# Decay sums of a gated delta-rule layer from bfloat16 parts instead of float32, with POOL writing their rows a phase ahead

## The chip, the cores and the metric

The kernel runs on one core of one Trainium2 chip. The metric is the device time of one execution, in microseconds (us). Engines are named as in the profile: PE is TensorE, PEld its weight loads, DVE is VectorE, ACT is ScalarE, POOL is GpSimd, SP is SyncE, which here issues the DMAs.

## The reference

One decoder layer on `x` (8 sequences of 128 tokens, 256 channels): a gated delta-rule attention with 8 heads, then a WKV mixer, then a mixture of 12 experts. The change touches the first part alone, and there the log decays:

```python
g = -jnp.exp(A_log) * jax.nn.softplus(x @ Wa.T + dt_bias)      # (B, L, H)
def step(state, inp):                                          # 2 steps per token, decay at the first
    state = state * jnp.exp(g_t)[..., None, None]
    corr = jnp.einsum('bhk,bhkv->bhv', k_t, state)
    state = state + jnp.einsum('bhk,bhv->bhkv', k_t, (v_t - corr) * b_t[..., None])
    o_t = jnp.einsum('bhk,bhkv->bhv', q_t, state)
```

The kernel doesn't step. It works on all 256 steps of a sequence at once, by matrices, and needs for every pair of steps the exponential of the sum of the `g` between them. A product of a 0/1 matrix with a matrix of `g` (its "decay rows") makes these sums.

## The kernel before, in words

The work goes head by head, in phases. Phase h (from -1 to 8) holds up to three things at once: the projections, convolutions and matrices of head h+1 ("new"), the start of the solve of head h ("now") and the rest of the solve and the output of head h-1 ("old"). The order of the steps on each engine is written out by hand: `TENSOR_ORDER`, `VECTOR_ORDER` and `SCALAR_ORDER` (lines 77 to 86) for phases 0 to 5, `FIRST_...` (lines 90 to 94) for phase -1, `NEXT_...` for phase 6, `LAST_...` and `FINAL_...` for the last two. A step with a prime belongs to head h-1.

Steps on PE, in the order of a phase: `0` to `9` are ten projections (L1290, each 4 records of 128x512), whose tiles ACT copies with the first tap (L592) and DVE convolves in three steps (L888, `u` in its order). A projection waits until DVE has done the third step of the projection two before it. `dt0`, `dt1` and `dt2` are the decay sums (L1337/L1338 for the first two, four sequences each; L1333/L1334 for the third). `ca`, `cs`, `nrm` sum squares, `e1_*`, `e2_*` are the products of keys (L1340, L1343), and `vt*` transposes. `mt0'`, `mm'`, `my1'` (L1359, L1364) merge blocks of the inverse, `w1`, `r2`, `w2`, `o` (L1476, L1478, L1480, L1482) apply it, `wo` (L1470) is the output projection and `ga` (L1466) the gate.

A decay sum is two matmuls that add up in PSUM: a float32 one (`seg`, a 0/1 matrix, times `Gb`) and a bfloat16 one (`segb` times `futb`, which puts a huge negative number on steps of the future). ACT takes the exponential of each tile (L631, L633 for `dt0` and `dt1`, L623, L624 for `dt2`).

POOL writes `Gb` with one instruction per head: the mask `lower` times `gl` of the head, repeated (L522, in `decay_rows`). For head 0 it comes at the end of a chain of small instructions in phase -1 (L502 to L516), and four small instructions for `beta` follow it (L526 to L529), on which DVE waits before its `rb` (L904). For head h+1, POOL first waits for `dt2` of head h on PE, since `Gb` is one buffer. Then it waits for `ly'` (L1439) and `yd` of head h and zeroes half of `Yc` (L535), which SP needs before the next scatter. Since these waits stand in one queue, `Gb` of head 2 and later is written in the phase that uses it, just behind L535.

Meanwhile DVE solves 16x16 blocks by substitution: 15 rounds per head of a multiply (L946, in the order an `s`) and a subtract (L953, another `s`), each of which reads two tensors in SBUF and waits for the one before. They are spread among `u`, `my0'`, `my1'` (L982), `r2_0'` and `r2_1'` (L985). `w2_0'` on PE waits for `r2_0'`. A convolution step reads one tensor from PSUM and one from SBUF.

Of the kernel before, what the change touches and what calls it, by code (L numbers as in the profile page):

```python
# [16 lines left out]
ALU = mybir.AluOpType  # L17
# [5 lines left out]
P = 128  # L23
# [19 lines left out]
class Signal:  # L43
# [10 lines left out]
    def next(self, name):  # L54
# [37 lines left out]
                "e1_5 e2_2 e1_6 e1_7 e2_3 vt0 vt1 vt2 vt3").split()  # L92
FIRST_TENSOR_ORDER = ("0 1 2 3 4 5 6 7 8 dt0 dt1 9 dt2 ca cs nrm e1_0 e1_1 e2_0 e1_2 e1_3 e2_1 e1_4 e1_5 e2_2 e1_6 e1_7 "
                "e2_3 vt0 vt1 vt2 vt3").split()
# [52 lines left out]
def build(nc, x, ctxt, w_qkv, w_gate, conv_w, w_ba, w_o, a_log, dt_bias, o_norm, t_decay, t_first,  # L147
          gate_w, w13, w2, consts, masks, y_init, expand, out):
    with ExitStack() as ctx:
# [30 lines left out]

        seg = sb("seg", [P, 2, P])
        segb = sb("segb", [P, 2, P], BF16)
        futb = sb("futb", [P, P], BF16)
        wba = sb("wba", [P, KC, 24])
        beta = sb("beta", [P, CH, H])
        bsig = sb("bsig", [P, CH, 2, H])
        gl = sb("gl", [P, B, H])
# [3 lines left out]
        tokb = sb("tokb", [P, B, 16])  # L191
        twice = sb("twice", [P, NH, P])
        al = sb("al", [P, H])
# [10 lines left out]
        xn = Vn2[0][:, :, :].rearrange("p c d -> p (c d)").rearrange("p (b c) -> p b c", b=B)  # L204
        Gb = sb("Gb", [P, B, L])
        DT2 = sb("DT2", [P, B, 192])
# [24 lines left out]
        T64 = sb("T64", [P, CH, 64])  # L231
        W1 = sb("W1", [P, B, D])
        R2 = sb("R2", [P, B, D])
        W2 = R2
# [79 lines left out]
        s_sq = Signal(sem("squares_ready"), ["0", "1"])  # L314
        s_gb = Signal(sem("decay_rows_ready"), ["gb"])
        s_yi = Signal(sem("solve_started_from_identity"), ["yi"], 16)
# [49 lines left out]
        def _(sp):  # L366
# [3 lines left out]
            for (dst, src), name in zip(first, s_first.names):  # L370
                sp.dma_start(dst, src).then_inc(s_first.next(name), 16)
            loads = [(seg[:, :, :], consts.rearrange("k p n -> p k n")[:, 6:8, :]), (cm[:, :], masks),
                     (al[:, :], a_log), (dtb[:, :], dt_bias),
# [98 lines left out]
        def _(pool):  # L472
# [43 lines left out]
            gt(gl[:, :, :], po, rep(al[:, :].rearrange("p (o h) -> p o h", o=1), 1, B), ALU.mult).then_inc(s_preG.next("gl"), 1)  # L516
            pool.wait_ge(s_preG.sem, s_preG.at("gl"))

            def decay_rows(h):

                hs = bass.ds(h, 1) if not isinstance(h, int) else slice(h, h + 1)
                g.tensor_tensor(Gb[:, :, :], rep(lower.rearrange("p (o l) -> p o l", o=1), 1, B), rep(gl[:, :, hs], 2, L), ALU.mult).then_inc(s_gb.next("gb"), 1)  # L522

# [4 lines left out]
            pk(gt(beta[:, :, :], beta[:, :, :], bsig[:, :, 0, :], ALU.add))  # L528
            gs(beta[:, :, :], beta[:, :, :], 2.0, None, ALU.mult).then_inc(s_preG.next("bparity"), 1)  # L529
            for h in range(H - 1):  # L530
                pool.wait_ge(prep.fills.sem, prep.fills.at("dt2", h))
                decay_rows(h + 1)
                pool.wait_ge(post.fills.sem, post.fills.at("ly", h))
                pool.wait_ge(s_yd.sem, s_yd.at("yd", h))
                g.tensor_tensor(Yc[:, :, SUB:BLK], T16[:, :, SUB:BLK], T16[:, :, SUB:BLK], ALU.add).then_inc(s_z.next("z"), 1)  # L535
# [281 lines left out]
        def _(dve):  # L817
# [50 lines left out]
            def gates():  # L868

                dve.wait_ge(s_first.sem, s_first.at("w_ba"))  # L870
                dve.wait_ge(s_ld.sem, 16 * N_LD)
                v.tensor_copy(segb[:, :, :], cst[:, 4:6, :])
                ts(futb[:, :], lower, BIG, -BIG, ALU.mult, ALU.add)

                dve.wait_ge(s_preA.sem, s_preA.at("gexp"))
                lk(ts(sm[2][:, :, :], sm[1][:, :, :], 2.0, None, ALU.add))
                v.reciprocal(sm[2][:, :, :], sm[2][:, :, :]).then_inc(s_preD.next("rr"), 1)
# [351 lines left out]
        def _(pe):  # L1229
# [72 lines left out]
            def prepare(name, h):  # L1302
                if name == "dt0":

                    pe.wait_ge(s_gb.sem, s_gb.at("gb", h))
                elif name == "ca":
                    pe.wait_ge(s_sq.sem, s_sq.at("0", h))
                elif name == "cs":
                    pe.wait_ge(s_sq.sem, s_sq.at("1", h))
                elif name == "nrm":  # L1310
                    pe.wait_ge(prep.emptied("cs").sem, prep.emptied("cs").at("cs", h))
                elif name == "e1_0":
                    pe.wait_ge(s_si.sem, s_si.at("u5", h))
                elif name == "vt0":
                    pe.wait_ge(s_si.sem, s_si.at(f"u{NU - 1}", h))
# [15 lines left out]
                elif name == "dt2":  # L1331
                    o = ps[:, :].rearrange("p (b l) -> p b l", b=B)
                    mm(o, seg[:, 1, :], Gb[:, :, 64:L], start=True, stop=False)  # L1333
                    ins = mm(o, segb[:, 1, :], rep(futb[:, 64:L].rearrange("p (o l) -> p o l", o=1), 1, B), start=False, stop=True)  # L1334
                elif name[:2] == "dt":
                    o = ps[:, :].rearrange("p (b l) -> p b l", b=4)
                    mm(o, seg[:, 0, :], Gb[:, 4 * i:4 * i + 4, :], start=True, stop=False)  # L1337
                    ins = mm(o, segb[:, 0, :], rep(futb[:, :].rearrange("p (o l) -> p o l", o=1), 1, 4), start=False, stop=True)  # L1338
# [336 lines left out]
```

## Time and profile before

| | before |
|---|---|
| median of three runs | 609.71 us (607.98 to 609.97) |
| the profiled execution's own time | 603.35 us |
| its span, first to last instruction | 601.6 us |
| mean granted TensorE clock in it | 0.972 of full |
| busy: PE, DVE, ACT, POOL | 557.3, 455.2, 357.8, 38.3 us |
| length of phases 1 to 4, by L535 | 59.2 to 59.4 us each |

A row of instructions reads: start, duration, engine, line, operation, what it writes <- what it reads, shapes, count; behind it in brackets how long the engine was idle before it, and who released it. Durations of PE's matmuls reach to the modelled end of each, so a stream of them overlaps; its pace is the distance between starts. A float32 matmul has two records.

### The profile page before, as it was taken

The page shows a single profiled execution, that of the slowest core. Times are in us where ns is not written, and L with a number is a line of the kernel's source. Part 1 is how long each engine was busy: PE and PEld are TensorE (multiplying, and loading weights), DVE is VectorE, ACT ScalarE, POOL GpSimd, SP SyncE. Part 2 cuts the span into 40 slices and gives each one's busy share as a digit, 9 for nine tenths or more (in the row PEclk, how much of TensorE's full clock was granted, in tenths as well). Part 3 has the DMA queues.
Part 4 walks back from the last instruction along what each step waited for, and adds up shares of the span by engine and source line. Part 5 has one row for each costly group of instructions (what it writes and reads, how often), then busy time and mean ns, then how long its engine had stood idle before and what let it go on. Part 6 is the DMA issues. An engine that isn't in the chain of part 4 may idle for free.

```text
span 601.6 us, 15363 instructions
## 1 busy us (share of the span) xinstructions
PE 557.3 (93%) x6484; PEld 377.7 (63%) x6484; DVE 455.2 (76%) x1066; ACT 357.8 (59%) x559; POOL 38.3 (6%) x66
## 2 busy tenths in 40 slices
PE   8799889999999999999999999999998799668997
PEld 5445347576657665766576667666666688556646
DVE  5778997797778877887788778878796535589663
ACT  2684766594659466946694668465864144187351
POOL 5340000100010001000100010010000000100000
PEclk9989999999999999999999999999998699968999
DMA  6001021102110200020002101210013400000002
GB/s 166 2 20 31 21 63 25 23 10 40 41 22 11 69 10 22 13 68 11 21 14 66 12 20 17 65 13 19 2 36 70 127 3 12 1 0 1 2 0 70
DMA packets 49700, 18.63 MB, mean 31 GB/s; under 512 B 39100, under 2 KB 48352, under 8 KB 49632
## 3 DMA queue, kind: packets, MB, share of 16 engines
q1 hardware_dynamic: 49632, 17.66, 12.2%
q8 instruction: 51, 0.84, 0.6%
q14 instruction: 17, 0.14, 0.1%
HBM read 14.49 MB, written 3.15 MB: 29 GB/s over the span
## 4 chain that ended last, share of the span: by engine, by line
PE 75%; DVE 11%; ACT 7%; issue 2%; SPq 1%; DMA 1%; POOL 0%; ACTq 0%; DVEq 0%
PE bank L1290 18%; PE bank L1340 7%; DVE acc L888 6%; PE bank L1470 4%; PE bank L1466 4%; PE bank L1238 4%; PE bank L1561 4%; PE bank L1343 3%; PE bank L1359 3%; PE bank L1482 3%; PE bank L1425 3%; PE bank L1476 3%; PE bank L1478 2%; PE bank L1480 2%; PE bank L1337 2%
## 5 line engine op out<-in xcount | busy, mean ns | idle before, releaser
L888 DVE SCALAR_TENSOR_TENSOR acc<-bank,cw,acc 128x508 f32<-128x508 f32 (+2 forms) x240 | 176.5, 739 | 36.3 <-ACT acc L592 32.1
L1290 PE MATMUL bank<-xnT,wq 128*128 128x512 f32 x320 | 154.9, 610 | 12.6 <-DVE acc L888 11.6
L1290 PEld LDWEIGHTS bank<-xnT,wq 128*128 128x128 f32 x320 | 56.3, 191 | 71.3 <-issue 43.4
L592 ACT ACTIVATE acc<-bank,cw 128x512 f32<-128x512 f32 x80 | 55.3, 691 | 52.7 <-PE bank L1290 50.4
L1340 PE MATMUL bank<-kq 128*128 128x384 f32 x128 | 49.9, 497 | 0.0
L639 ACT ACTIVATE T<-bank 32x512 f32<-32x512 f32 (+1 forms) x32 | 18.9, 590 | 41.9 <-PE bank L1359 29.0
L607 ACT ACTIVATE vT<-acc 128x512 f32<-128x512 f32 x32 | 21.0, 671 | 37.5 <-DVE acc L888 37.4
L921 DVE SCALAR_TENSOR_TENSOR AM<-bank,rb,DT 128x384 f32<-128x384 f32 x64 | 37.6, 608 | 1.8 <-PE bank L1340 1.5
L989 DVE SCALAR_TENSOR_TENSOR xres<-bank,f,xres 128x256 f32<-128x256 f32 x64 | 26.9, 478 | 8.6 <-PE bank L1470 8.3
L607 ACT ACTIVATE kq<-acc 128x512 f32<-128x512 f32 x48 | 31.6, 660 | 2.2 <-DVE acc L888 1.9
L1470 PE MATMUL bank<-wo,oTh 128*128 128x256 f32 x128 | 31.9, 383 | 0.0
L1466 PE MATMUL bank<-xnT,wg 128*128 128x512 f32 x64 | 30.3, 595 | 0.0
L535 POOL TENSOR_TENSOR Yc<-T 128x256 f32<-128x256 f32 x7 | 4.3, 611 | 403.8 <-PE bank L1439 403.8
L663 ACT ACTIVATE Yd<-Yc 32x512 f32<-32x512 f32 x32 | 20.1, 628 | 16.5 <-DVE Xc L974 16.2
L1343 PEld LDWEIGHTS bank<-kq 128*128 128x128 f32 x128 | 22.1, 190 | 10.5 <-issue 3.1
L607 ACT ACT_TABLE_LOAD x22 | 28.2, 1283 | 0.4
L1340 PEld LDWEIGHTS bank<-kq 128*128 128x128 f32 x128 | 22.3, 190 | 9.6 <-issue 2.2
L1482 PE MATMUL bank<-AM,W 128*128 128x128 f32 x128 | 28.2, 302 | 0.0
L953 DVE TENSOR_TENSOR Yl<-Yl,tmp 128x15 f32<-128x15 f32 (+7 forms) x120 | 25.2, 210 | 3.9
L946 DVE TENSOR_TENSOR tmp<-Yl,Bl 128x15 f32<-128x15 f32 (+7 forms) x120 | 24.2, 201 | 5.1 <-DMA Bl<-blocks 3.0
L1470 PEld LDWEIGHTS bank<-wo,oTh 128*128 128x128 f32 x128 | 23.7, 190 | 6.1 <-issue 1.2
L1343 PE MATMUL bank<-kq 128*128 128x192 f32 x128 | 26.0, 326 | 0.0
(247 smaller groups left out, 1085.1 us busy)
## 6 DMA issues: line engine op xcount, KB each, us to landing
wq<-in_w_qkv SPq DMA_DIRECT2D x8, 640.0 KB, 4.1
blocks<-AM SPq DMA_DIRECT2D x128, 8.0 KB, 1.5
xres<-in_x SPq DMA_DIRECT2D x2, 512.0 KB, 4.5
Yl<-in_y_init SPq DMA_DIRECT2D x8, 128.0 KB, 2.4
Bl<-blocks SPq DMA_DIRECT2D x8, 128.0 KB, 2.0
wg<-in_w_gate SPq DMA_DIRECT2D x8, 128.0 KB, 2.1
solved<-Yl SPq DMA_DIRECT2D x8, 128.0 KB, 1.7
Yc<-solved SPq DMA_DIRECT2D x64, 16.0 KB, 1.9
```

Source lines behind the costliest of these rows:

```text
L592: a(acc[:, u % RING, :, :], bank[6 + u % 2][:, :].rearrange("p (b l) -> p b l", b=4), ACT.Copy, scale=cw[:, t, 3:4]).then_inc(s_tap.next(f ...
L607: a(dst, src, ACT.Silu).then_inc(s_si.next(f"u{u}"), 1)
L888: stt(w, ps[:, :, 0:L - s], cw[:, t, 3 - s:4 - s], w, ALU.mult, ALU.add).then_inc(s_cv.next(f"u{u}_{s}"), 1)
L921: stt(AM1[:, b, :], prep.tile(name)[:, 0:KQ], rb[:, b:b + 1], DT1[:, b, :], ALU.mult, ALU.mult).then_inc(prep.emptied(name).next(name), 1)
L953: tt(y, y, t, ALU.subtract).then_inc(s_so.next(f"{k}s"), 1)
L989: ins = stt(xx, ring.tile(name)[:, C * j:C * j + C], f4[:, 2 * k + j:2 * k + j + 1], xx, ALU.mult, ALU.add)
L1290: ins = mm(bank[6 + u % 2][:, :], wq[:, cc, t, :], xnT[:, cc, 512 * half:512 * half + 512], start=cc == 0, stop=cc == KC - 1)
L1340: ins = mm(ps[:, 0:KQ], kq[:, i, 0:P], kq[:, i, :], start=True, stop=True)
L1343: ins = mm(ps[:, 192 * k:192 * k + 192], kq[:, b, 2 * P:3 * P], kq[:, b, 192:KQ], start=True, stop=True)
L1466: ins = mm(ps[:, :], wg[:, cc, :], xnT[:, cc, 512 * k:512 * k + 512], start=cc == 0, stop=cc == KC - 1)
L1470: ins = mm(ps[:, C * j:C * j + C], oTh[:, L * b:L * b + L], wo[:, :], start=True, stop=True)
L1482: mm(o, W1[:, b, :], AM1[:, b, P:2 * P], start=True, stop=True)
```

## The change

- The log decays `gl` are split once, in phase -1 on POOL, into three bfloat16 parts that add up to the float32 number (`gl3`): five small instructions, one after the other.
- `Gb` is now bfloat16 and holds the three parts. `decay_rows` writes it with six instructions of 128x512 instead of one of 128x1024: for each half of the batch three parts, with a signal behind each half.
- Each of the three decay tiles is made of three bfloat16 matmuls with `pastb` (a bfloat16 copy of `seg`, made by DVE in phase -1) instead of the float32 one, and the bfloat16 one with `futb` as before. `dt0` waits for the first half and `dt1` for the second.
- POOL writes the rows of head h+2 as soon as `dt2` of head h+1 is done, ahead of its wait for `ly'` of head h.
- In phase -1, `dt1` stands behind projection 9 on PE.
- `twice`, `seg` and `bsig` share memory with `W1`.

```diff
-FIRST_TENSOR_ORDER = ("0 1 2 3 4 5 6 7 8 dt0 dt1 9 dt2 ca cs nrm ...
+FIRST_TENSOR_ORDER = ("0 1 2 3 4 5 6 7 8 dt0 9 dt1 dt2 ca cs nrm ...
...
-        Gb = sb("Gb", [P, B, L])
+        Gb = sb("Gb", [P, 3, B, L], BF16)
+        gl3 = sb("gl3", [P, 3, B, H], BF16)
...
+        twice = W1[:, 0:NH, :]
+        seg = W1[:, 4:6, :]
+        bsig = W1[:, 6:8, :].rearrange("p k (c n h) -> p (k c) n h", n=2, h=H)
...
-        s_gb = Signal(sem("decay_rows_ready"), ["gb"])
+        s_gb = Signal(sem("decay_rows_ready"), ["0", "1"])
...
             pool.wait_ge(s_preG.sem, s_preG.at("gl"))
+            pk(g.tensor_copy(gl3[:, 0, :, :], gl[:, :, :]))
+            pk(gt(r2, gl[:, :, :], gl3[:, 0, :, :], ALU.subtract))
+            pk(g.tensor_copy(gl3[:, 1, :, :], r2))
+            pk(gt(r2, r2, gl3[:, 1, :, :], ALU.subtract))
+            pk(g.tensor_copy(gl3[:, 2, :, :], r2))
 
             def decay_rows(h):
 
                 hs = bass.ds(h, 1) if not isinstance(h, int) else slice(h, h + 1)
-                g.tensor_tensor(Gb[:, :, :], rep(lower..., 1, B), rep(gl[:, :, hs], 2, L), ALU.mult).then_inc(s_gb.next("gb"), 1)
+                for f in range(2):
+                    bs = slice(4 * f, 4 * f + 4)
+                    for part in range(3):
+                        i = g.tensor_tensor(Gb[:, part, bs, :], rep(lower..., 1, 4), rep(gl3[:, part, bs, hs], 2, L), ALU.mult)
+                    i.then_inc(s_gb.next(str(f)), 1)
...
+            pool.wait_ge(prep.fills.sem, prep.fills.at("dt2", 0))
+            decay_rows(1)
             for h in range(H - 1):
-                pool.wait_ge(prep.fills.sem, prep.fills.at("dt2", h))
-                decay_rows(h + 1)
+                if h + 2 < H:
+                    pool.wait_ge(prep.fills.sem, prep.fills.at("dt2", h + 1))
+                    decay_rows(h + 2)
                 pool.wait_ge(post.fills.sem, post.fills.at("ly", h))
                 pool.wait_ge(s_yd.sem, s_yd.at("yd", h))
...
                 v.tensor_copy(segb[:, :, :], cst[:, 4:6, :])
+                v.tensor_copy(pastb[:, :, :], seg)
...
-                if name == "dt0":
-                    pe.wait_ge(s_gb.sem, s_gb.at("gb", h))
+                if name in ("dt0", "dt1"):
+                    pe.wait_ge(s_gb.sem, s_gb.at(name[2], h))
...
-                    mm(o, seg[:, 1, :], Gb[:, :, 64:L], start=True, stop=False)
+                    for part in range(3):
+                        mm(o, pastb[:, 1, :], Gb[:, part, :, 64:L], start=part == 0, stop=False)
...
-                    mm(o, seg[:, 0, :], Gb[:, 4 * i:4 * i + 4, :], start=True, stop=False)
+                    for part in range(3):
+                        mm(o, pastb[:, 0, :], Gb[:, part, 4 * i:4 * i + 4, :], start=part == 0, stop=False)
```

## Rows read from the trace of the kernel before

**Rows 1.** Stretch, length, busy PE, PEld, DVE, ACT, POOL, clock; phase 0, phase 2.

```profile
48.00:108.00 60.00, 54.66 (x629) 31.49 (x627) 51.18 (x115) 35.82 (x56) 0.00 (x0) 1.00 0.15 30
167.20:226.50 59.30, 58.28 (x757) 39.58 (x757) 48.39 (x111) 38.83 (x60) 2.48 (x2) 1.00 0.13 28
```

**Rows 2.** PE in order of time, phase 2, around the decay tiles.

```profile
171.40 1.02 PE L1337 MATMUL bank<-Gb,seg 128*128 128x512 f32 x2
172.26 0.38 PE L1338 MATMUL bank<-futb,segb 128*128 128x512 bf16 x1
172.48 0.17 PE L1235 MATMUL bank<-segb 128*128 128x1 bf16 x1
...
173.65 1.12 PE L1337 MATMUL bank<-Gb,seg 128*128 128x512 f32 x2
174.61 0.38 PE L1338 MATMUL bank<-futb,segb 128*128 128x512 bf16 x1
174.82 0.19 PE L1235 MATMUL bank<-segb 128*128 128x1 bf16 x2
...
179.01 1.13 PE L1333 MATMUL bank<-Gb,seg 128*128 128x512 f32 x2
179.97 0.38 PE L1334 MATMUL bank<-futb,segb 128*128 128x512 bf16 x1
180.19 1.95 PE L1476 MATMUL bank<-Vn,Yd 128*128 128x128 f32 x16
...
185.54 1.88 PE L1290 MATMUL bank<-xnT,wq 128*128 128x512 f32 x4
187.26 1.95 PE L1480 MATMUL bank<-R,Yd 128*128 128x128 f32 x16
```

**Rows 3.** The chain of waits in order of time, end of phase -1 (start, us, what).

```profile
39.12 0.86 PE bank L1337 x2
...
43.02 0.69 ACT acc L592
```

**Rows 4.** POOL in order of time, phases -1 and 2, and one DVE instruction between.

```profile
32.10 0.32 POOL L516 TENSOR_TENSOR gl<-sm,al 128x64 f32<-128x64 f32 x1
32.50 1.92 POOL L522 TENSOR_TENSOR Gb<-cst,gl 128x1024 f32<-128x1024 f32 x1
36.89 0.53 POOL L529 TENSOR_SCALAR beta<-beta 128x128 f32<-128x128 f32 x1
47.74 0.19 DVE L904 TENSOR_TENSOR rb<-ri,beta 128x16 f32<-128x16 f32 x1
167.22 0.61 POOL L535 TENSOR_TENSOR Yc<-T 128x256 f32<-128x256 f32 x1 [56.72 <-PE bank L1439]
```

**Rows 5.** DVE, its convolution while POOL writes rows in phase 2, then in the rest of the phase.

```profile
L888 DVE SCALAR_TENSOR_TENSOR acc<-bank,cw,acc x3: 736/739/743, 167.2 to 168.8; 128x508 f32<-128x508 f32 x1, 128x504 f32<-128x504 f32 x1, 128x500 f32<-128x500 f32 x1
L888 DVE SCALAR_TENSOR_TENSOR acc<-bank,cw,acc x27: 701/741/748, 171.5 to 225.9; 128x508 f32<-128x508 f32 x9, 128x504 f32<-128x504 f32 x9, 128x500 f32<-128x500 f32 x9
```

**Rows 6.** DVE in order of time, phase 2, behind the decay tiles.

```profile
180.22 0.21 DVE L953 TENSOR_TENSOR Yl<-Yl,tmp 128x48 f32<-128x48 f32 x1
180.35 0.68 DVE L982 TENSOR_SCALAR Yd<-bank 64x512 f32<-64x512 f32 x1
180.95 0.72 DVE L888 SCALAR_TENSOR_TENSOR acc<-bank,cw,acc 128x500 f32<-128x500 f32 x1
181.59 0.20 DVE L946 TENSOR_TENSOR tmp<-Yl,Bl 128x55 f32<-128x55 f32 x1
...
182.49 2.30 DVE L888 SCALAR_TENSOR_TENSOR acc<-bank,cw,acc 128x508 f32<-128x508 f32 x3
184.70 0.22 DVE L946 TENSOR_TENSOR tmp<-Yl,Bl 128x63 f32<-128x63 f32 x1
...
185.10 0.68 DVE L985 TENSOR_TENSOR R<-Vn,bank 128x512 f32<-128x512 f32 x1
```

**Rows 7.** PE in order of time, phase 0: a projection behind a wait on DVE.

```profile
73.74 1.98 PE L1290 MATMUL bank<-xnT,wq 128*128 128x512 f32 x4 [0.86 <-DVE acc L888]
```

More of the change, by code:

```diff
@@ L92 @@
                 "e1_5 e2_2 e1_6 e1_7 e2_3 vt0 vt1 vt2 vt3").split()
-FIRST_TENSOR_ORDER = ("0 1 2 3 4 5 6 7 8 dt0 dt1 9 dt2 ca cs nrm e1_0 e1_1 e2_0 e1_2 e1_3 e2_1 e1_4 e1_5 e2_2 e1_6 e1_7 "
+FIRST_TENSOR_ORDER = ("0 1 2 3 4 5 6 7 8 dt0 9 dt1 dt2 ca cs nrm e1_0 e1_1 e2_0 e1_2 e1_3 e2_1 e1_4 e1_5 e2_2 e1_6 e1_7 "
                 "e2_3 vt0 vt1 vt2 vt3").split()
@@ L179, in build @@
         vT = sb("vT", [P, B, 2 * L])
-        seg = sb("seg", [P, 2, P])
+        pastb = sb("pastb", [P, 2, P], BF16)
         segb = sb("segb", [P, 2, P], BF16)
@@ L185, in build @@
         beta = sb("beta", [P, CH, H])
-        bsig = sb("bsig", [P, CH, 2, H])
         gl = sb("gl", [P, B, H])
@@ L191, in build @@
         tokb = sb("tokb", [P, B, 16])
-        twice = sb("twice", [P, NH, P])
         al = sb("al", [P, H])
@@ L371, in _ @@
                 sp.dma_start(dst, src).then_inc(s_first.next(name), 16)
-            loads = [(seg[:, :, :], consts.rearrange("k p n -> p k n")[:, 6:8, :]), (cm[:, :], masks),
+            loads = [(seg, consts.rearrange("k p n -> p k n")[:, 6:8, :]), (cm[:, :], masks),
                      (al[:, :], a_log), (dtb[:, :], dt_bias),
@@ L517, in _ @@
             pool.wait_ge(s_preG.sem, s_preG.at("gl"))
+            pk(g.tensor_copy(gl3[:, 0, :, :], gl[:, :, :]))
[3 more added lines that the diff above has]
+            pk(g.tensor_copy(gl3[:, 2, :, :], r2))
             def decay_rows(h):
                 hs = bass.ds(h, 1) if not isinstance(h, int) else slice(h, h + 1)
-                g.tensor_tensor(Gb[:, :, :], rep(lower.rearrange("p (o l) -> p o l", o=1), 1, B), rep(gl[:, :, hs], 2, L), ALU.mult).then_inc(s_gb.next("gb"), 1)
+                for f in range(2):
+                    bs = slice(4 * f, 4 * f + 4)
+                    for part in range(3):
+                        i = g.tensor_tensor(Gb[:, part, bs, :], rep(lower.rearrange("p (o l) -> p o l", o=1), 1, 4), rep(gl3[:, part, bs, hs], 2, L), ALU.mult)
+                    i.then_inc(s_gb.next(str(f)), 1)
             decay_rows(0)
```

## The prediction

> **What bounds the kernel now.** I began with the busy time by stretch [rows 1]. In phase 2 PE is busy 58.28 of 59.30 us and DVE 48.39, at the full clock of 2.4 GHz, so each microsecond that PE is spared in such a phase can shorten the span. By the table above phases 1 to 4 are of one length, and I take 5 and 6 to be like them. Phase 0 is another matter: PE is busy 54.66 of 60 us and DVE 51.18, and a projection stands idle 0.86 us for a convolution [rows 7]. There DVE and ACT set the pace. Then I read PE in order of time around the decay tiles [rows 2], the end of phase -1 [rows 3], POOL [rows 4], and DVE, both where POOL now works [rows 5] and where it will work [rows 6]. POOL does 2.48 us in a phase of 59; it is the free engine.
>
> **PE's saving.** A decay tile is a float32 matmul in two records and a bfloat16 one. From start to start the first takes 0.86 us (171.40 to 172.26) and the second 0.22 (172.26 to 172.48) [rows 2]. The new tile is four bfloat16 matmuls, 4 x 0.22 = 0.88 us. Of the old tiles `dt0` takes 1.08, `dt1` 1.17 (173.65 to 174.82) and `dt2` 1.18 (179.01 to 180.19), the last two behind small matmuls, where their float32 weight load is not hidden. So a phase saves 0.20 + 0.29 + 0.30 = 0.8 us; were the first load still exposed by 0.09 us, 0.6. In phases 1 to 6 that is on the path: 6 x 0.8 = 4.8 us (3.6 at least). What is late next: `mm'` behind `dt1` waits for ACT's copy of `mt0'`, but that copy moves up with PE as well. In phase 0 I count nothing, since the wait of rows 7 would grow by what PE saves.
>
> In phase -1 projection 9 comes one tile earlier on PE, by 0.88 and 0.2 us. ACT takes its tile at 43.02 [rows 3] and is then free of the exponentials of `dt0` 0.3 us earlier, not more: a gain of 0.3 us.
>
> **POOL in phase -1.** Five small instructions at 0.32 us, as L516, and 0.08 between, make 2.0 us; they hold back all that POOL does behind them. A row instruction has 512 columns. The nearest rows are 0.61 us for 256 and 1.92 for 1024 [rows 4]; between them 1.0 us, bounds 0.95 and 1.1. So the rows stand at 32.5 + 2.0 + 3.0 = 37.5 and, second half, 40.5; DVE's copy `pastb` (some 0.28 us) can move both by as much. `dt0` starts at about 39.1 [rows 3] and `dt1` will start behind projection 9, at about 41.5. Both are in time, and this is why `dt1` could be moved. The four instructions for `beta` ended at 37.4 [rows 4] and now end at 43; DVE reads `beta` at 47.74 (L904). Cost: nothing, covered by 4 us. If the copy were not hidden, 0.3 us.
>
> **POOL later.** L535 and SP behind it keep their place, and no DMA moves. The new waits for `dt2` of head h+1 stand ahead of L535 of head h, but `dt2` comes half a phase before `ly'`; a burst of 6 us is long over. The next `dt0` is 50 us away. By the order of events nothing is late.
>
> **What lies beside the burst.** This is the step on which the sign hangs. POOL used to write for 1.9 us beside L888: DVE's convolution then took 736 to 743 ns, against 701 to 748 elsewhere [rows 5]. L888 reads one tensor in SBUF. The burst now begins when `dt2` is done, about 179.6 on the clock of phase 2, and lasts to 185.6 at least. There DVE is in its substitution [rows 6], pairs of L946 and L953, each with two SBUF tensors, as POOL's own instruction has. No row of the trace shows the two side by side. Bounds: below, no cost, as rows 5 have it; above, each of the six POOL instructions holds DVE for its 1.0 us once, 6 us a phase. A gain is excluded. I take a value between: whenever DVE comes from an instruction with one SBUF tensor back to a pair, it waits for the POOL instruction in progress, 0.9 us of its 1.0. I take this rather than zero because the rows at zero are of another form, and DVE's form is the one that needs a second stream from SBUF.
>
> The Trainium skill, page "SBUF — State Buffer", section "Who interferes with whom", states such a rule: a DVE instruction with two SBUF inputs contends with a POOL instruction that reads SBUF, and the second to start is held until the first is done, while one with one input is not. By its second half rows 5 agree; by a strict reading of the first, the sum would be near my upper bound, and without the rule it would be the gain of 5 us alone.
>
> Worked out for phase 2. DVE is 0.5 us early when the burst begins, PE 0.8. Returns to a pair come at 180.22, 181.59 and 184.70 [rows 6], less 0.5. The first two lie before the convolution of projection 4 (L888 x3 at 182.49, done at 184.8, now 184.3): 1.8 us make 186.1. Projection 6 waits for that; it stood at 185.54 [rows 2] and would start at 184.7. So PE waits 1.4 us, against 0.8 saved: +0.6. The third return (0.7) puts `r2_0'` (L985 at 185.10, done 185.8) at 187.8, and `w2_0'`, at 187.26 + 0.6, just doesn't wait more. Five phases (1 to 5) give +3.0. In phase 0 the burst meets the same pairs, and DVE has no slack: three waits, of which I count 2.2 us. In phase -1 the burst of head 1 lies at 43.5 to 49.5, beside one small two-tensor instruction on the path to `e1_0`, L904 [rows 4]: +0.5, against the 0.3 gained. Phase 6 has no burst: -0.8.
>
> **Sum**: 3.0 + 2.2 + 0.5 - 0.3 - 0.8 = +4.6 us on the profiled execution's 603.35 (a span of 601.6 and 1.75 around it), so 608.0. The median of the runs is 609.71, 6.4 us above that execution; I add the difference to the median: **614.3 us**.
>
> **The rivals.**
> - *PE's gain undisturbed* (the other side). DVE and POOL don't touch each other, as in rows 5. Then -4.8 - 0.3 = -5.1: 604.6 us. For it: PE is the full engine, the substitution has small instructions, and POOL ran beside DVE without a mark wherever it did. Against: only the one-tensor form was seen. It decides from the point where the three waits before projection 6 come to less than 0.4 us in all. Chance 0.34.
> - *Absorbed.* The waits are there but short, some 1.2 us before projection 6, and PE's slack there (0.5 us and the 0.8 saved set against each other) takes most: 608 to 611.5 us, in the middle 610. Also here: parts of the PE gain lost to another wait. Chance 0.18.
> - *Turn by turn to the full.* POOL gets in at each gap between two instructions of a pair. Then the pairs up to projection 4's convolution wait for five POOL instructions, 4.7 us, DVE is done with it at 189.0 instead of 184.3, PE waits 4.3, net +3.5 in each of five phases, +3.5 in phase 0, +0.5, -0.3, -0.8: +20.4, or 630.1 us. Against it: the pair at 184.70 has done its two 0.22 us by 185.10 [rows 6], with no gap to get in. Chance 0.2, and 0.28 for my forecast's own range of 611.5 to 620; together these two are one mechanism, DVE held by POOL, at 0.48, the likeliest.
> - *Not what it says*: three bfloat16 matmuls that share one weight matrix could be slower than the one with `futb` shows. They would need 0.29 us each for the saving to vanish; the row says 0.22. Under 0.02, left inside "absorbed".
>
> **How the numbers follow.** The time is that of DVE held by POOL, 614.3. The range goes from 604.5, the undisturbed gain with all of its 0.8 us a phase, to 630, the full turns; some 1 in 10 is left out on either side, below for timed runs that gain more, above for a POOL that holds DVE through the whole burst. 0.3% is 1.8 us, about what a measurement of this kernel can tell from no change: below 607.9 is faster, above 611.5 slower. Faster: 0.34 of the undisturbed gain and 0.01. Slower: 0.48 and 0.01. Same: 0.16.
>
> **What would show each step.** L1337 three records of bfloat16, tiles 0.88 us from start to start. `dt1` in phase -1 without a wait for POOL. Beside L522, L946 and L953 last 0.2 us (undisturbed) or up to 1.0 us or more (held), or stand idle; in the waits, PE L1290 for DVE L888 near projection 6 of phases 1 to 5 grows from nothing. Phases measured from L535 to L535 would be 58.5 us (undisturbed), 59.9 (mine) or 62.8 (full turns), and phase 6 is 0.8 us shorter in all. I am wrong if L946 and L953 keep their durations.

## The result, and the profile after

The changed kernel takes 634.06 us (median of four runs, 633.0 to 636.31), the kernel before 608.85 us beside it (607.56 to 609.97). The ratio is 1.0431, with a 95% interval of 1.0384 to 1.0478: slower by 4.3%. Forecast were 614.3 us, slower, in a range of 604.5 to 630. The sign was right; the size and the range were not. Some executions of one and the same kernel run longer at a lower granted clock; the ratios here and below leave them out, among them one of 914.02 us at 0.554.

| | before | after |
|---|---|---|
| profiled execution, its own time / span | 603.35 / 601.6 us | 633.24 / 631.2 us |
| mean granted clock in it | 0.972 | 0.946 |
| busy DVE | 455.2 us | 477.0 us |
| busy POOL | 38.3 us | 73.4 us |
| mean length of phases 1 to 5, by the instruction on `Yc` | 59.0 us | 62.7 us |

Lines have moved: L888 is now L904 (convolution), L946 is L962 and L953 is L969 (substitution), L982 is L998, L1290 is L1306 (projections), L1337 is L1355, L1333 is L1350, L1338 is L1356, L1334 is L1351, L522 is L533 (rows), L535 is L550.

The prediction had named two marks of a DVE that is held: substitution instructions of up to 1.0 us, and PE waiting for a convolution. DVE in order of time, after, in the phase that answers to [rows 6]:

```profile
189.01 0.21 DVE L962 TENSOR_TENSOR tmp<-Yl,Bl 128x48 f32<-128x48 f32 x1
189.25 1.02 DVE L969 TENSOR_TENSOR Yl<-Yl,tmp 128x48 f32<-128x48 f32 x1
190.20 0.67 DVE L998 TENSOR_SCALAR Yd<-bank 64x512 f32<-64x512 f32 x1
190.80 0.72 DVE L904 SCALAR_TENSOR_TENSOR acc<-bank,cw,acc 128x500 f32<-128x500 f32 x1
191.45 0.85 DVE L962 TENSOR_TENSOR tmp<-Yl,Bl 128x55 f32<-128x55 f32 x1
192.33 0.97 DVE L969 TENSOR_TENSOR Yl<-Yl,tmp 128x55 f32<-128x55 f32 x1
193.34 0.98 DVE L962 TENSOR_TENSOR tmp<-Yl,Bl 128x60 f32<-128x60 f32 x1
194.35 0.97 DVE L969 TENSOR_TENSOR Yl<-Yl,tmp 128x60 f32<-128x60 f32 x1
195.25 2.29 DVE L904 SCALAR_TENSOR_TENSOR acc<-bank,cw,acc 128x508 f32<-128x508 f32 x3
```

POOL in the same stretch, and PE behind it:

```profile
189.17 6.08 POOL L533 TENSOR_TENSOR Gb<-cst,gl 128x512 bf16<-128x512 f32 x6 [11.79 <-PE bank L1351]
```

```profile
188.05 0.82 PE L1350 MATMUL bank<-Gb,pastb 128*128 128x512 bf16 x3
188.71 0.38 PE L1351 MATMUL bank<-futb,segb 128*128 128x512 bf16 x1
188.92 1.95 PE L1494 MATMUL bank<-Vn,Yd 128*128 128x128 f32 x16
...
197.59 1.71 PE L1306 MATMUL bank<-xnT,wq 128*128 128x512 f32 x3 [2.83 <-DVE acc L904]
```

This is the whole case in a few rows. POOL's six instructions take 6.08 us. Each is recorded as 1.05 us long and they start 1.01 us apart, so by that pace they end at 190.22, 191.22, 192.23, 193.24, 194.24 and 195.25. The five stretched DVE instructions end at 190.27, 192.30, 193.30, 194.32 and 195.32: each 0.05 to 0.08 us behind the end of a POOL instruction. They are long not because they compute, but because each is held until POOL's current instruction is done. Between them stand L998 and L904, each with its usual time [rows 6]; they read PSUM, and at most one tensor of SBUF. The five take 4.79 us against the 1.06 of undisturbed ones (0.21, 0.20, 0.22, 0.22, 0.22): DVE is held 3.7 us. The convolution of projection 4 ends 3.7 us later for it. PE waits 2.83 us ahead of projection 6, so some 0.9 us of the delay are covered by what PE had to spare there.

DVE's rows show no idle time there. The holding is inside the durations, so it can't be found in the list of waits of DVE, only in the mean durations of the page. These are its groups of the two instructions, and PE's wait:

```profile
L1306 PE MATMUL bank<-xnT,wq 128*128 128x512 f32 x320 | 159.7, 627 | 30.0 <-DVE acc L904 29.0
L969 DVE TENSOR_TENSOR Yl<-Yl,tmp 128x15 f32<-128x15 f32 (+7 forms) x120 | 37.8, 315 | 3.9
L962 DVE TENSOR_TENSOR tmp<-Yl,Bl 128x15 f32<-128x15 f32 (+7 forms) x120 | 32.9, 274 | 7.2 <-DMA Bl<-blocks 5.2
```

They come from a second profile of the changed kernel (`e9_changed_again`, below); the first has 318 ns for L969 and 272 for L962. In the kernel before the means were 210 and 201 ns, and PE's idle time behind DVE's convolutions 11.6 us.

**Where the 29.6 us between the two profiled spans lie**, by the starts of the instruction on `Yc` (before: 108.02, 402.90 and 464.80 us for the first, sixth and seventh; after: 113.73, 427.15, 489.46). Up to the first: 5.7. Phases 1 to 5: 18.5. Phase 6, which has no burst: 0.4. The rest: 4.9 (the terms are rounded). The first and the last term are partly TensorE's clock, which the second profile tells apart. Its starts are 111.46, 426.28 and 489.30, in a span of 626.2: 3.4 + 19.9 + 1.1 + 0.1 = 24.6 us over the span before. So the 4.9 us at the end don't belong to the change, as experiment `e9_changed_again` shows, and some 2 of the 5.7 at the start don't either.

### The profile page after: what moved, and what is told of

Its sections match the earlier page's. It is cut to its first block, busy times and chain, and to the rows that moved or that the text cites. A ratio compares the mean times of both kernels' runs of the same rounds, so it can differ in the third digit from the quotient of the medians.

```text
span 631.2 us, 15457 instructions
## 1 busy us (share of the span) xinstructions
PE 567.2 (90%) x6500; PEld 385.1 (61%) x6508; DVE 477.0 (76%) x1067; ACT 358.3 (57%) x559; POOL 73.4 (12%) x111
## 4 chain that ended last, share of the span: by engine, by line
PE 66%; DVE 21%; ACT 6%; issue 4%; SPq 1%; DMA 1%; POOL 0%; ACTq 0%; DVEq 0%
PE bank L1306 15%; DVE acc L904 9%; PE bank L1358 7%; PE bank L1488 4%; PE bank L1484 4%; DVE Yl L969 4%; PE bank L1254 3%; PE bank L1579 3%; PE bank L1361 3%; PE bank L1500 3%; PE bank L1377 3%; DVE tmp L962 3%; PE bank L1443 3%; PE bank L1498 3%; ACT acc L607 2%
## 5 line engine op out<-in xcount | busy, mean ns | idle before, releaser
L904 DVE SCALAR_TENSOR_TENSOR acc<-bank,cw,acc 128x508 f32<-128x508 f32 (+2 forms) x240 | 176.3, 738 | 38.1 <-ACT acc L607 33.7
L1306 PE MATMUL bank<-xnT,wq 128*128 128x512 f32 x320 | 161.5, 632 | 30.1 <-DVE acc L904 28.9
L1306 PEld LDWEIGHTS bank<-xnT,wq 128*128 128x128 f32 x320 | 57.7, 196 | 90.9 <-issue 44.9
L533 POOL TENSOR_TENSOR Gb<-cst,gl 128x512 bf16<-128x512 f32 x48 | 48.7, 1049 | 80.5 <-PE bank L1351 80.4
L550 POOL TENSOR_TENSOR Yc<-T 128x256 f32<-128x256 f32 x7 | 4.3, 619 | 318.4 <-PE bank L1457 318.4
L969 DVE TENSOR_TENSOR Yl<-Yl,tmp 128x15 f32<-128x15 f32 (+7 forms) x120 | 38.1, 318 | 3.9
L654 ACT ACTIVATE R<-bank 128x512 f32<-128x512 f32 x32 | 19.1, 596 | 32.9 <-PE bank L1498 27.7
L962 DVE TENSOR_TENSOR tmp<-Yl,Bl 128x15 f32<-128x15 f32 (+7 forms) x120 | 32.6, 272 | 6.4 <-DMA Bl<-blocks 4.3
L1488 PE MATMUL bank<-wo,oTh 128*128 128x256 f32 x128 | 34.6, 407 | 0.0
L1488 PEld LDWEIGHTS bank<-wo,oTh 128*128 128x128 f32 x128 | 25.3, 204 | 6.7 <-issue 1.2
L1361 PEld LDWEIGHTS bank<-kq 128*128 128x128 f32 x128 | 22.1, 190 | 10.4 <-issue 3.1
```

The source lines that it names most:

```text
L533: i = g.tensor_tensor(Gb[:, part, bs, :], rep(lower.rearrange("p (o l) -> p o l", o=1), 1, 4), rep(gl3[:, part, bs, hs], 2, L), ALU.mult)
L904: stt(w, ps[:, :, 0:L - s], cw[:, t, 3 - s:4 - s], w, ALU.mult, ALU.add).then_inc(s_cv.next(f"u{u}_{s}"), 1)
L962: tt(t, rep(Yl[:, 0:rows, k:k + 1], 2, cols), rep(Bl[:, k:k + 1, k + 1:SUB], 1, rows), ALU.mult).then_inc(s_so.next(f"{k}m"), 1)
L969: tt(y, y, t, ALU.subtract).then_inc(s_so.next(f"{k}s"), 1)
L1306: ins = mm(bank[6 + u % 2][:, :], wq[:, cc, t, :], xnT[:, cc, 512 * half:512 * half + 512], start=cc == 0, stop=cc == KC - 1)
L1361: ins = mm(ps[:, 192 * k:192 * k + 192], kq[:, b, 2 * P:3 * P], kq[:, b, 192:KQ], start=True, stop=True)
```

## The experiments

The theory behind the first ones: POOL's reads of SBUF hold each of DVE's two-tensor instructions until the current POOL instruction ends, and this is the whole of the loss. The rivals: DVE is held by POOL's writes; the loss is in something else that the change moved (the new order of POOL's queue, the shared memory, the bfloat16 tiles); the price lies in the number of POOL's instructions rather than their time.

### The rows behind the substitution

```diff
                 if h + 2 < H:
                     pool.wait_ge(prep.fills.sem, prep.fills.at("dt2", h + 1))
+                    pool.wait_ge(s_so.sem, s_so.at(f"{SUB - 2}s", h))
                     decay_rows(h + 2)
```

`s_so` at this name is the last subtraction of the substitution of head h. The rows of head 1 stay where they were.

> The changed kernel, but POOL starts the rows of head h+2 only when the last substitution round of head h is done (some 12 us after dt2), where DVE runs convolutions again. If DVE is held by POOL's instructions (my theory), L962 and L969 are back at 0.2 us each, the waits of projection 6 for DVE are gone, and the saving on PE is left alone: 5 us below the kernel before, near 604 us (0.990 to 0.995 of it). If the loss comes from the bfloat16 decay tiles, the shared memory or phase -1, it stays near 634 us, since all of that is unchanged.

Measured: 606.58 us against 609.03 of the kernel before, ratio 0.9935 (0.9899 to 0.9971). The profiled execution was the one at a clock of 0.554, so the kernel was profiled once more:

> The kernel with the rows behind the substitution once more, for a profile at the usual clock. My theory: L970 and L963 at 0.2 us, no wait of projection 6 for DVE in phases 1 to 5, these phases at 58.5 to 59.0 us (the run without bursts had 58.8), span near 600 us. If the burst holds DVE at its new place as well, phases of 59.5 us or more.

Measured: 606.93 us, with a span of 605.1; the 600 expected of the span was missed, and 5 us of that lie behind phase 6, where the clock was low (below). POOL, and DVE around it, in that profile:

```profile
191.71 6.09 POOL L533 TENSOR_TENSOR Gb<-cst,gl 128x512 bf16<-128x512 f32 x6 [24.15 <-DVE Yl L970]
```

```profile
191.38 0.19 DVE L970 TENSOR_TENSOR Yl<-Yl,tmp 128x15 f32<-128x15 f32 x1
191.47 0.74 DVE L905 SCALAR_TENSOR_TENSOR acc<-bank,cw,acc 128x504 f32<-128x504 f32 x1
192.12 0.75 DVE L1029 SCALAR_TENSOR_TENSOR oTh<-bank,onw,gate 128x512 f32<-128x512 f32 x1
...
195.00 2.30 DVE L905 SCALAR_TENSOR_TENSOR acc<-bank,cw,acc 128x508 f32<-128x508 f32 x3 [1.49 <-ACT acc L608]
```

The same six instructions, of the same 6.09 us, lie beside instructions that read one tensor in PSUM, and none of these is stretched. (In phase 0 the moved burst does meet one small instruction with two tensors in SBUF: `rb` takes 0.83 us instead of 0.19 and ends at 86.69, 0.05 us behind the burst.) The five phases take 58.3 us each (58.29, 58.88, 58.39, 59.02, 57.15). Everything else of the change is still in this kernel, so the loss of 25 us hangs on this one overlap. The new wait costs nothing: the next `dt0` is some 30 us away. And this version is faster than both kernels, than the one before by 0.65% (0.3 to 1.0).

### No rows, and rows that are only written

Rows of heads 1 to 7 not written at all (two small memsets carry the signals):

```diff
             def decay_rows(h):
...
+                if h:
+                    for f in range(2):
+                        g.memset(raw2[:, f:f + 1], 0.0).then_inc(s_gb.next(str(f)), 1)
+                    return
```

> The changed kernel without the row instructions of heads 1 to 7: each head then multiplies with the rows of head 0, so its output isn't the reference's; PE, DVE and ACT do all that they did. If POOL's burst is the cause, this is the pure gain on PE, about 5 us below the kernel before (604 us), and phases 1 to 5 last 58.5 us from L535 to L535. If the PE part is the cause, it stays near 634 us. If it is 604 and the run with the rows behind the substitution is slower than this one, the burst costs something at its new place too.

Measured: 605.9 us, ratio 0.9962 (0.9924 to 1.0001), 2 us above what was expected and not clearly apart from the kernel before. Phases of 58.8, 58.8, 59.1, 58.7 and 57.6 us.

Rows replaced by twelve memsets of 128x512, which write and read nothing:

```diff
+                if h:
+                    for again in range(2):
+                        for f in range(2):
+                            for part in range(3):
+                                i = g.memset(Gb[:, part, 4 * f:4 * f + 4, :], 0.0)
...
+                    return
```

> The changed kernel, but for heads 1 to 7 POOL fills the row buffer twice with zeros by twelve memsets instead of multiplying: it writes SBUF and reads nothing, at the same place for 3 to 6 us. The decays of these heads are left out, so the output isn't the reference's. If only POOL's reads hold DVE, L962 and L969 stay at 0.2 us and the time is near 604 us. If any POOL work holds them, or its writes do, single ones are stretched as in the changed kernel, and the time lies above 615 us.

Measured: 598.77 us in one run, 5 us less than expected. In that profile 130.6 us lie behind the last instruction on `Yc`, against 136.8 before, so the surplus isn't in the phases compared here. POOL, then DVE where it was held in the changed kernel:

```profile
180.73 5.78 POOL L534 MEMSET Gb<- 128x512 bf16 x12 [11.77 <-PE bank L1361]
```

```profile
180.84 0.21 DVE L979 TENSOR_TENSOR Yl<-Yl,tmp 128x48 f32<-128x48 f32 x1
...
182.21 0.20 DVE L972 TENSOR_TENSOR tmp<-Yl,Bl 128x55 f32<-128x55 f32 x1
182.44 0.21 DVE L979 TENSOR_TENSOR Yl<-Yl,tmp 128x55 f32<-128x55 f32 x1
...
182.95 0.22 DVE L979 TENSOR_TENSOR Yl<-Yl,tmp 128x60 f32<-128x60 f32 x1
```

A burst of almost the same length in the same place holds nobody. So it is POOL's reads that hold DVE, not its writes and not its being busy.

### Reads of one tensor

The six instructions as copies of `gl3`, repeated, without the mask:

```diff
+                if h:
...
+                            i = g.tensor_copy(Gb[:, part, bs, :], rep(gl3[:, part, bs, hs], 2, L))
...
```

> The changed kernel, but for heads 1 to 7 POOL only copies the bfloat16 parts, spread over 512 columns, in the same six pieces: one tensor read instead of two. The mask is left out, so the output isn't the reference's. If any POOL instruction that reads SBUF holds a DVE instruction with two SBUF tensors, each copy still stretches one of L962 and L969 to its own length (0.5 to 1 us): 612 to 634 us. If it takes two tensors on either side, none is stretched and the time is near 604 us.

Measured: 607.2 us in one run, beside 610.71 of the kernel before. The holding is there as expected, but the time lies below the 612 to 634 that were expected with it. POOL and DVE:

```profile
180.61 3.39 POOL L534 COPY Gb<-gl 128x512 bf16<-128x512 bf16 x6 [11.77 <-PE bank L1358]
```

```profile
180.71 0.57 DVE L976 TENSOR_TENSOR Yl<-Yl,tmp 128x48 f32<-128x48 f32 x1
...
182.45 0.49 DVE L969 TENSOR_TENSOR tmp<-Yl,Bl 128x55 f32<-128x55 f32 x1
182.97 0.53 DVE L976 TENSOR_TENSOR Yl<-Yl,tmp 128x55 f32<-128x55 f32 x1
183.54 0.53 DVE L969 TENSOR_TENSOR tmp<-Yl,Bl 128x60 f32<-128x60 f32 x1
```

One input is enough on POOL's side. The copies start some 0.56 us apart, and four DVE instructions take 0.49 to 0.57: again about one POOL instruction each. They lose 1.3 us together, and the phases lengthen by only 0.6 us against the kernel with the rows behind the substitution: the longest wait of PE for a convolution in phases 1 to 5 is 0.7 us here, against 2.8 in the changed kernel.

### The same rows in longer and shorter pieces

Three instructions of 128x1024, and twelve of 128x256:

```diff
+                if h:
+                    for part in range(3):
+                        i = g.tensor_tensor(Gb[:, part, :, :], rep(lower..., 1, B), rep(gl3[:, part, :, hs], 2, L), ALU.mult)
...
```

```diff
+                if h:
...
+                            for c in range(2):
+                                bs = slice(4 * f + 2 * c, 4 * f + 2 * c + 2)
+                                i = g.tensor_tensor(Gb[:, part, bs, :], rep(lower..., 1, 2), rep(gl3[:, part, bs, hs], 2, L), ALU.mult)
...
```

With three pieces both signals come behind the last one.

> The changed kernel, but for heads 1 to 7 with three row instructions of 128x1024 instead of six of 128x512, the same rows. If a DVE instruction waits for the end of the whole POOL instruction, fewer of L962 and L969 are stretched, but each to some 1.9 us, and the sum of the stretching per phase is again 3.5 to 5 us: a time of 625 to 640 us. If POOL and DVE share piece by piece, the instructions that meet a burst last as long as in the changed kernel (about 1 us) whatever the length of POOL's.

> The changed kernel, but for heads 1 to 7 twelve row instructions of 128x256 per head instead of six of 128x512. If DVE waits for the end of whichever POOL instruction is in progress and POOL gets the next turn, more of L962 and L969 are stretched, each to 0.5 to 0.6 us, and the sum per phase is like that of the six: 3 to 4.5 us, time 622 to 640 us. If only long POOL instructions hurt, the stretching is gone and the time is below 612 us.

Measured: 628.33 and 619.51 us, one run each. DVE with three long pieces:

```profile
190.69 1.89 DVE L975 TENSOR_TENSOR Yl<-Yl,tmp 128x48 f32<-128x48 f32 x1
...
193.75 0.71 DVE L968 TENSOR_TENSOR tmp<-Yl,Bl 128x55 f32<-128x55 f32 x1
194.49 1.84 DVE L975 TENSOR_TENSOR Yl<-Yl,tmp 128x55 f32<-128x55 f32 x1
```

And with twelve short ones:

```profile
185.37 0.59 DVE L977 TENSOR_TENSOR Yl<-Yl,tmp 128x48 f32<-128x48 f32 x1
...
187.13 0.56 DVE L970 TENSOR_TENSOR tmp<-Yl,Bl 128x55 f32<-128x55 f32 x1
187.72 0.54 DVE L977 TENSOR_TENSOR Yl<-Yl,tmp 128x55 f32<-128x55 f32 x1
188.29 0.55 DVE L970 TENSOR_TENSOR tmp<-Yl,Bl 128x60 f32<-128x60 f32 x1
188.87 0.54 DVE L977 TENSOR_TENSOR Yl<-Yl,tmp 128x60 f32<-128x60 f32 x1
...
191.78 0.52 DVE L977 TENSOR_TENSOR Yl<-Yl,tmp 128x63 f32<-128x63 f32 x1
```

The held time follows the pace of POOL's instructions (one per 1.9, 1.01 and 0.58 us): three turns and 3.8 us with long pieces, five and 3.7 as changed, six and 2.0 with short ones. With short pieces I had expected 3 to 4.5 us, since the burst as a whole is longer (6.95 us). That was wrong: DVE's instructions between the held ones that read PSUM run beside POOL's and use up its burst, and a turn costs only what is left of one short instruction beyond DVE's own 0.2 us. In phase 2 of each of these kernels the held instructions end 0.05 to 0.08 us behind the end of a POOL instruction, by POOL's pace in each.

### The kernel before, with only the queue's new order

The one float32 instruction of the kernel before, a phase ahead:

```diff
             for h in range(H - 1):
-                pool.wait_ge(prep.fills.sem, prep.fills.at("dt2", h))
-                decay_rows(h + 1)
+                if h + 2 < H:
+                    pool.wait_ge(prep.fills.sem, prep.fills.at("dt2", h + 1))
+                    decay_rows(h + 2)
```

> The kernel before, all in float32, with one edit: POOL's single row instruction (1.9 us) is started a phase ahead, behind dt2, as in the change. If the place beside the substitution is what costs, one or two of L946 and L953 per phase are stretched, by up to 1.9 us in all instead of none, and since projection 6 has 0.75 us to spare for DVE, phases 1 to 5 grow by 0 to 1.2 us each: 609 to 616 us. If the loss needed the bfloat16 rows or the three-part matmuls, the durations stay at 0.2 us and the time at that of the kernel before.

Measured: 613.41 us against 610.71, ratio 1.0055 (1.0009 to 1.0101). POOL and DVE:

```profile
182.81 1.91 POOL L522 TENSOR_TENSOR Gb<-cst,gl 128x1024 f32<-128x1024 f32 x1 [12.60 <-PE bank L1337]
```

```profile
183.33 0.72 DVE L891 SCALAR_TENSOR_TENSOR acc<-bank,cw,acc 128x500 f32<-128x500 f32 x1
183.97 0.82 DVE L949 TENSOR_TENSOR tmp<-Yl,Bl 128x55 f32<-128x55 f32 x1
184.83 0.22 DVE L956 TENSOR_TENSOR Yl<-Yl,tmp 128x55 f32<-128x55 f32 x1
```

One DVE instruction is held, from 183.97 until 0.07 us behind the end of POOL's at 184.72; the rest of the 1.9 us lies beside instructions that read PSUM. So the holding needs neither the bfloat16 parts nor six pieces. It costs nothing in phases 1 to 5, which are as long as before (59.01 us, with 0.6 us held in each). This profile's span is 8.2 us above that of the kernel before: 2.0 us lie ahead of the first instruction on `Yc` (110.02 instead of 108.02), 2.2 in phase 6 and 3.9 behind it, both without a burst. That the small loss of the medians (0.55%, at least 0.09%) comes from the holding is thus not shown.

### VectorE's delay without POOL

The kernel with the rows behind the substitution, and one instruction that only takes time, ahead of the convolution of projection 4:

```diff
+                if u == 4 and s == 1 and delayed[0] in range(1, 7):
+                    v.reduce_max(held[:, delayed[0]:delayed[0] + 1], rep(held[:, 0:1], 1, 3500), axis=AX)
...
```

> The kernel with the rows after the substitution (606.6 us), and in phases 0 to 5 one more VectorE instruction, of 3.7 us, ahead of the convolutions of projection 4 of the next head. It reads one SBUF tensor, writes a tile of its own, and POOL is not beside it. Nothing is left out. Theory, the price of the burst is VectorE's delay alone: PE stalls some 2.8 us ahead of projection 6 in each of phases 0 to 5, phases of 61.5 to 63 us from L535's counterpart to the next, time 625 to 635 us as the changed kernel, and a granted clock below that of the kernel before. Rival, holding by POOL costs something besides the delay (PE or the transfers are disturbed as well): the stall is there, but the time stays at 615 to 622 us.

> The changed kernel once more, on the chip of the run with the inserted delay. 630 to 637 us, with VectorE in five turns with POOL in each of phases 0 to 5, the last of the three convolutions of projection 4 ending some 3.7 us late, and PE stalled 2.8 us. If the 5 us by which its last phase is longer than that of the kernel before come from the change, they are there again; if from TensorE's clock in that one execution, the last phase is 57 to 60 us here.

Measured on one chip: 633.32 us (628.13 to 636.54) with the delay, 632.75 (628.19 to 636.65) for the changed kernel, and 611.88 (600.12 to 613.79) for the kernel before; the ratios to the kernel before are 1.033 (1.0242 to 1.0419) and 1.0346 (1.0262 to 1.0431). DVE and PE with the delay:

```profile
191.72 3.79 DVE L903 TENSOR_REDUCE held<-held 128x1 f32<-128x3500 f32 x1
195.43 2.29 DVE L912 SCALAR_TENSOR_TENSOR acc<-bank,cw,acc 128x508 f32<-128x508 f32 x3
```

```profile
197.77 1.98 PE L1314 MATMUL bank<-xnT,wq 128*128 128x512 f32 x4 [3.13 <-DVE acc L912]
```

Six delays of 3.79 us, with POOL's burst elsewhere, give the loss of the changed kernel to within the intervals of 1%. The rival (a cost of the holding besides the delay) had 615 to 622 us and falls. Four of the five phases with the delay are longer than the 61.5 to 63 us that were expected (63.84, 61.99, 63.59, 64.50, 63.42), since the clock fell in them.

### The held time against the length of a phase

Put side by side, from the profiles (held: the stretched instructions of phase 2 less their undisturbed time; phase: mean of phases 1 to 5):

| kernel | held, us | phase, us |
|---|---|---|
| before | 0 | 58.98 |
| no rows | 0 | 58.60 |
| memsets | 0 | 58.38 |
| rows behind the substitution | 0 | 58.35 |
| six copies | 1.3 | 59.00 |
| twelve short | 2.0 (1.7 ahead of the convolution) | 59.77 |
| six, as changed (two profiles) | 3.7 | 62.68, 62.96 |
| three long | 3.8 | 62.75 |
| a delay of 3.79 | 3.8 | 63.47 |

The first 1.3 us costs little (0.4 to 0.65 us a phase against the kernels without a burst or with a harmless one). From 1.7 to 3.7 us of holding the phase grows by 3 us, more than the 2 us between them. The second profile of the changed kernel shows what comes on top. Stretches from one instruction on `Yc` to the next (start, end, length, busy time and count of PE, PEld, DVE, ACT, POOL, granted clock, DMA):

```profile
175.43:239.07 63.64, 59.53 (x759) 40.45 (x760) 52.18 (x111) 38.86 (x60) 6.70 (x7) 0.97 0.12 26
239.07:301.28 62.21, 57.99 (x759) 39.53 (x760) 52.08 (x111) 38.83 (x60) 6.69 (x7) 1.00 0.13 27
301.28:365.29 64.01, 59.64 (x759) 40.80 (x760) 52.17 (x111) 39.00 (x60) 6.69 (x7) 0.97 0.12 26
```

DVE's work is the same in all three. In two of them the clock's mean is 0.97 and PE is busy 1.5 us longer. Directly behind PE's gap of 2.83 us (it ends at 196.26) the granted clock was 0.64 of full, so part of the time at 1.2 GHz. In the middle one it stayed at 2.4 GHz behind a gap of 2.83 us too (it ends at 259.89):

```profile
196.00:200.00 4.00, 3.74 (x9) 2.14 (x10) 3.86 (x12) 0.00 (x0) 0.00 (x0) 0.64 0.01 4
260.00:263.00 3.00, 3.00 (x16) 2.04 (x17) 2.89 (x9) 0.20 (x1) 0.00 (x0) 1.00 0.02 5
```

In the kernel with the rows behind the substitution, without the gap, the clock was 1.00 in each of phases 1 to 5. So in these phases the clock falls only in kernels in which PE has the gap, but not at each gap, and it adds some 1.5 us where it does. With the inserted delay it fell in four of five phases, which is why its phases are the longest. With the twelve short pieces, where PE's longest wait is 1.1 us, it fell in none. What decides in which phases it falls stays open.

The stretch behind phase 6 is another matter. From the last instruction on `Yc` to POOL's next one it is, in the kernel before, in the changed one, in the kernel with the rows behind the substitution, and in the second profile of the changed one:

```profile
464.80:522.06 57.26, 49.90 (x817) 43.60 (x817) 27.33 (x71) 17.77 (x32) 0.61 (x1) 0.91 0.15 45
```

```profile
489.46:551.75 62.29, 56.14 (x817) 48.07 (x817) 27.07 (x70) 17.77 (x32) 0.67 (x1) 0.81 0.13 41
```

```profile
463.04:525.30 62.26, 55.77 (x817) 48.10 (x817) 26.68 (x69) 17.77 (x32) 0.61 (x1) 0.81 0.13 40
```

```profile
489.30:546.76 57.46, 50.06 (x817) 43.67 (x817) 27.16 (x71) 17.77 (x32) 0.63 (x2) 0.91 0.14 44
```

The 5 us go with the clock (0.81 or 0.91), and the clock goes with the execution, not with the kernel: the changed kernel shows both, and the kernel with the rows behind the substitution shows the low one. A reader of the first pair of profiles alone would have put a sixth of the loss down to the change. From the last instruction on `Yc` to the end of the span it is 136.8 us before, 141.7 and 136.9 in the two profiles after.

## Why the prediction was wrong in size

**The bound and PE's saving.** The new tile is 0.88 us from start to start, as said: 188.05, 188.71, 188.92 above for `dt2`. What reaches the phase is less than the 0.8 us said: without any burst a phase is 0.4 us shorter (58.98 to 58.60), with the harmless burst 0.6. Part of it went to another wait that I had not named, PE's sequencer ahead of the small matmuls of `tb` (L1425 before): six waits of 3.8 us in all between 105 and 470 us before, of 5.3 without the burst. Mis-sized by 0.2 to 0.4 us a phase. Phase 6 was said to be 0.8 us shorter and was 0.4 and 1.1 longer in the two profiles; its clock was 0.97 before and 0.95 in both.

**POOL in phase -1** went as predicted: `dt1` has no wait for the rows, `beta` was done in time, and DVE's `rb` took 0.28 us instead of 0.19, where +0.5 had been counted. `rb` has two tensors in SBUF and did lie beside the burst of head 1 (45.30 to 51.38). It was held for only 0.1 us because it came near the end of a POOL instruction, and ended 0.04 us behind it (49.41 against 49.37 by POOL's pace). That was luck; where it met the burst in phase 0 of the kernel with the moved rows, it cost 0.64 us.

**What lies beside the burst** is the step that failed, word for word: "I take a value between: whenever DVE comes from an instruction with one SBUF tensor back to a pair, it waits for the POOL instruction in progress". That made three waits a phase, two of 0.9 us and one of 0.7, only two of them ahead of projection 6. The runs show a wait for every instruction of a pair that meets the burst, five in phase 2 and all five ahead of projection 6: 3.7 us instead of 1.8. The argument against the full turns was "no gap to get in", since the two instructions of a pair follow each other closely. But POOL's instructions stand back to back in its queue. A held DVE instruction ends 0.05 to 0.08 us behind a POOL instruction, and its successor, which needs its result, starts 0.02 to 0.03 us later (192.30 to 192.33, 193.31 to 193.34), when the next POOL instruction has started. So POOL's burst isn't longer for it (6.08 us beside the substitution, 6.09 beside the convolutions), and DVE is held again.

The prediction's premise was wrong too: "No row of the trace shows the two side by side". One row of the kernel before did. POOL's own instruction on `Yc` reads SBUF, and behind phase 6 it meets a subtract of the substitution:

```profile
464.80 0.61 POOL L535 TENSOR_TENSOR Yc<-T 128x256 f32<-128x256 f32 x1 [59.42 <-PE bank L1439]
```

```profile
464.82 0.63 DVE L953 TENSOR_TENSOR Yl<-Yl,tmp 128x28 f32<-128x28 f32 x1
```

The subtract of this shape takes 0.19 us elsewhere; here it takes 0.63 and ends 0.04 us behind POOL's instruction. This row contradicts the rival with the largest chance, 0.34, the undisturbed gain, for which the prediction said that POOL ran beside DVE "without a mark wherever it did". It can't say how many turns a burst of six would take, as it has one POOL instruction only.

**The rival "turn by turn to the full"** had this mechanism, five turns, 4.7 us and a chance of 0.2; 630.1 us was 4 us short of the median. It counted 4.7 us held and 4.3 of waiting where 3.7 and 2.83 were measured, since a held instruction's own 0.2 us is no loss, and it counted nothing for the clock. Measured are 61.9 to 62.4 us in those of phases 1 to 4 in which the clock stayed at 1.00, and 63.0 to 64.2 where it fell; without any burst these four take 58.7 to 59.1. In phase 3 of the second profile (62.21 us, clock 1.00) the difference to a phase without a burst (58.81) is 3.4 us, and the starts of PE's instructions show it whole. `r2` (L1496) starts 0.32 us later behind its predecessor, since it waits for L998, the instruction behind the first held one. Projection 6 starts 2.99 us later; the 2.83 in the profile's brackets count only from the modelled end of the matmul before. `w2` (L1498) starts 0.10 us later behind that. So such a phase is 2.9 us longer than before the change (59.3), not the rival's 3.5. That its sum comes near is partly luck: it has 17.5 us for phases 1 to 5, where 18.5 and 19.9 were measured, because waits counted too long stand against a clock that was not counted at all, some 1.5 us in each of three phases.

**Phase 0**: +2.2 us for DVE and +0.2 for phase -1 were said; the second profile shows 3.4 us up to the first instruction on `Yc`, and PE's waits for convolutions in phase 0 are 7.9 us instead of 4.4.

**The page.** The Trainium skill, "SBUF — State Buffer", section "Who interferes with whom", says that a DVE instruction with two SBUF inputs contends with a POOL instruction that reads SBUF, and not with one that only writes. This case's runs agree with each half: 0.85 to 1.02 us beside the reading instructions, 0.20 to 0.22 beside the memsets, and no mark on instructions with one SBUF input (L904 takes 0.72 us beside the burst). I had weighed it, and then taken a value below its strict reading on the strength of rows of another form [rows 5]. Its strict reading, priced per DVE instruction, was the better guide.

**The range** ended at 630 us, the sum of the full turns. Past that the time is carried by the clock, some 4.5 us in three phases, and by phase 6, which did not gain 0.8 us: the forecast priced each microsecond of waiting as one microsecond.

## What to carry to other kernels

- Look for the longest duration of each line in the trace you have, not only for its mean: L953 has a median of 209 ns and one row of 630, and that row was the missing evidence.
- Before a POOL instruction that reads SBUF is moved, count the DVE instructions with two SBUF inputs that will lie beside it. Each is held to the end of the POOL instruction in progress, so DVE loses at most their number times the rest of one POOL instruction, and at most the burst; the kernel loses what of this the engine behind DVE can't cover. Put the burst beside work that reads PSUM, or make its pieces short; here one more wait, on the last round of the substitution, turned a loss of 4.3% into a gain of 0.65% (0.3 to 1.0) over the kernel before.
- Holding doesn't show as waiting. Look for it where the mean duration of a form has grown (201 to 272 ns) and its work has not.
- A stall of PE can cost more than its length, since the clock may fall behind it; and a clock that differs between two profiles should be seen in a second profile of the same kernel before its cost is given to the change.

## What the runs showed of the hardware that I had not expected

- POOL's side needs one SBUF input only: copies, one per 0.56 us, hold DVE as the two-input instructions do.
- The turns are one-sided. A back-to-back burst on POOL was not slowed (six instructions in 6.08 us beside the substitution, in 6.09 away from it), while a chain of dependent 0.2 us instructions on DVE ran at POOL's pace: one per 1.01, 0.58 or 1.9 us. A single POOL instruction was lengthened a little where a two-tensor DVE instruction had started with or just before it: the one on `Yc` at 489.46 took 0.67 us instead of 0.61.
- The granted clock fell behind a gap of 2.8 us of PE in some phases and not in others of the same execution, and one stretch with the same 817 matmul records came at 0.91 in 57 us or at 0.81 in 62.
